# Scores and state products in halves of TensorE's array, and the chunk output made turned, in one bank with the carried part

## The reference

```python
x = silu(causal_conv(x_in @ Wx.T));  z = x_in @ Wz.T            # 512 channels
b = (x @ Wb.T).reshape(bsz, seq, 8, 64);  c = (x @ Wc.T).reshape(bsz, seq, 8, 64)
dt = softplus(x @ Wdt.T + b_dt);  a = -exp(log_a)
def step(state, (x_t, b_t, c_t, dt_t)):                         # over 1024 tokens
    state = exp(dt_t * a) * state + (dt_t * b_t)[..., None] * x_t[:, :, None, :]
    y_t = einsum('bhn,bhnp->bhp', c_t, state)
y = y + d_param * x;  y = (y - mean_head) / sqrt(var_head + eps) * gn_w + gn_b
out = (y * silu(z)) @ Wout.T
# second half: gelu(h @ (alpha1*sign(w1)).T + b1) @ (alpha2*sign(w2)).T + b2
```

## Time and profile before

| | |
|---|---|
| median of three runs | 1528.94 us (1528.52 to 1531.23) |
| the profiled execution | 1531.44 us, its span 1529.7 us |
| mean granted TensorE clock | 0.974 |
| TensorE busy | 1426.4 us, 93% of the span |
| its weight loads | 986.9 us, 65% |
| VectorE | 1092.1 us, 71% |
| ScalarE | 828.8 us, 54% |
| GpSimd | 439.2 us, 29% |

### The profile page before, as it was taken

How to read it: one execution, slowest core, us unless ns; L and a number is a source line. 1 busy time by engine, 2 the same in 40 slices (tenths; PEclk the granted TensorE clock), 3 DMA queues, 4 the chain that set the end, 5 groups by cost and what they waited for, 6 DMA issues and landing times.

```text
span 1529.7 us, 28256 instructions
## 1 busy us (share of the span) xinstructions
PE 1426.4 (93%) x9712; PEld 986.9 (65%) x9712; DVE 1092.1 (71%) x2424; ACT 828.8 (54%) x1718; POOL 439.2 (29%) x487
## 2 busy tenths in 40 slices
PE   4999999998999989999999999999899999999776
PEld 3484758676485856758577675867658585675654
DVE  5454786858777686876859678685877769586665
ACT  3555574555745475553746447454674547555231
POOL 2020242214331232313422134321333134321343
PEclk8899999999999999999999999999999999999888
DMA  6000000101000010100001010010100000000000
GB/s 225 1 15 1 15 1 1 42 1 44 1 15 28 2 44 1 42 1 16 29 1 43 1 44 1 2 42 1 44 1 17 26 1 28 1 28 1 28 1 28
DMA packets 33351, 33.22 MB, mean 22 GB/s; under 512 B 4888, under 2 KB 31640, under 8 KB 33184
## 3 DMA queue, kind: packets, MB, share of 16 engines
q1 hardware_dynamic: 33184, 31.11, 6.2%
HBM read 22.72 MB, written 8.39 MB: 20 GB/s over the span
## 4 chain that ended last, share of the span: by engine, by line
PE 66%; issue 14%; DVE 10%; POOL 5%; ACT 2%; SPq 1%; DMA 0%; POOLq 0%; DVEq 0%; ACTq 0%
PE bank L1291 20%; PE bank L1473 7%; PE bank L1460 7%; PE bank L1377 6%; PE bank L1410 5%; PE bank L1445 4%; PE bank L1389 4%; PE bank L1369 3%; PE bank L1397 3%; PE bank L1359 2%; PE bank L1361 2%; SPq L548 1%; PE bank L1301 1%; DVE un L937 1%; POOL yT L670 1%
## 5 line engine op out<-in xcount | busy, mean ns | idle before, releaser
L686 POOL TENSOR_TENSOR xdw<-xdt,decays 128x512 f32<-128x512 f32 x64 | 66.7, 1043 | 430.3 <-DVE xdt L1043 408.1
L1291 PE MATMUL bank<-sh,WbT 128*128 128x512 f16 x768 | 174.3, 383 | 10.3 <-DVE sh L967 10.1
L1291 PE MATMUL bank<-sh,WcT 128*128 128x512 f16 x768 | 175.5, 379 | 0.0
L881 ACT ACTIVATE yk<-bank,decays 128x64 f32<-128x64 f32 x512 | 112.1, 330 | 86.4 <-PE bank L1389 86.4
L962 DVE SCALAR_TENSOR_TENSOR xs<-xi,taps,xs 128x512 f32<-128x512 f32 x192 | 152.5, 805 | 8.7 <-ACT xs L787 4.4
L1473 PE MATMUL bank<-sign2T,hh 128*128 128x256 f16 x1024 | 151.2, 275 | 2.0 <-DVE hh L1157 2.0
L868 ACT ACTIVATE mt<-bank 128x512 f32<-128x512 f32 x128 | 69.5, 596 | 148.3 <-PE bank L1361 148.3
L1410 PE MATMUL bank<-xdt,mt 128*128 128x64 f32 x1024 | 142.9, 262 | 0.0
L1291 PEld LDWEIGHTS bank<-sh,WbT 128*128 128x128 f16 x768 | 73.6, 98 | 100.6 <-issue 14.5
L1410 PEld LDWEIGHTS bank<-xdt,mt 128*128 128x128 f32 x1024 | 134.9, 192 | 2.2
L1291 PEld LDWEIGHTS bank<-sh,WcT 128*128 128x128 f16 x768 | 75.1, 98 | 87.1
(11 more groups left out here) (182 smaller groups left out, 2755.1 us busy)
## 6 DMA issues: line engine op xcount, KB each, us to landing
xt<-L_attn_input_tensor_dram SPq DMA_DIRECT2D x16, 512.0 KB, 4.8
u<-L_attn_input_tensor_dram SPq DMA_DIRECT2D x16, 512.0 KB, 3.7
out_dram<-u SPq DMA_DIRECT2D x16, 512.0 KB, 3.0
yT<-in_L_ffn_w_dram SPq DMA_DIRECT2D x2, 1024.0 KB, 14.1
zs<-in_L_attn_Wb_dram SPq DMA_DIRECT2D x1, 1024.0 KB, 8.6
zs<-in_L_attn_Wc_dram SPq DMA_DIRECT2D x1, 1024.0 KB, 10.8
BT<-in_L_attn_Wx_dram SPq DMA_DIRECT2D x1, 512.0 KB, 4.7
BT<-in_L_attn_Wz_dram SPq DMA_DIRECT2D x1, 512.0 KB, 6.1
```

Source lines behind the costliest of these rows:

```text
L686: pool.tensor_tensor(xdw[n % 2][:, :, :], xdt[n % 2][:, :, :], per_head(decays[:, 1, q, :]), ALU.mult)\
L881: last = nc.scalar.activation(yk[n % 2][:, h, :], bank(t, ("YI", j, q))[:, h * HD:(h + 1) * HD], ACT.Copy, scale=decays[:, 0, q, h:h + 1])
L1291: mm = nc.tensor.matmul(bank(t, key)[:, :], w[i][:, k, cols(m)], v[h][:, k, :], start=(a == 0), stop=(a == len(terms) - 1))
```

## The change

It is made of these edits, all at once:

1. Scores: the eight S matmuls alternate between the two halves of rows (g = 0, 1 inside the loop over c); both banks are waited for before the first.
2. State product: St becomes eight matmuls, one a head, with 64 columns of weights and 64 moving, written to 64 partitions of the bank; the unused products go.
3. Chunk output: Y is made turned. The weights are `xdt` of a head (64 columns), `mt` moves (128 columns), the result goes to 64 partitions of the bank, and it is added to YI, which now is made turned too, with `state` as weights, in the same bank ("Y" begins in `carry`, ends in `back`).
4. Since YI can no longer be scaled by ScalarE afterwards, C is scaled before: a new fp16 matmul "E" of 512 columns over 64 rows at the end of `front`, an exponential of it on ScalarE into `Cd`, and a product with C on GpSimd, in front of YI.
5. `turn`, the eight scalings of L881, the addition of L1066 and the third of the decay sums (L1347) go; of VectorE's steps the addition to `yT` alone is left, and it is done in `back`.
6. The masks have other shapes: of_target halves, of_source doubles.

```diff
@@ turn_steps @@
-        steps += own(("turn", j, 0)) + [(who, "in_norm", nj)] + own(("front", j, 3)) + [(who, "xT", nj, 0)]
-        steps += tail(("end_stat", j)) + own(("carry", j, 2), ("back", j, 2), ("turn", j, 1)) + [(who, "xT", nj, 1)]
-        steps += tail(("end_root", j), ("end_norm", j)) + own(("carry", j, 3), ("turn", j, 2), ("back", j, 3))
+        steps += [(who, "in_norm", nj)] + own(("front", j, 3)) + [(who, "xT", nj, 0)]
+        steps += tail(("end_stat", j)) + own(("carry", j, 2), ("back", j, 2)) + [(who, "xT", nj, 1)]
+        steps += tail(("end_root", j), ("end_norm", j)) + own(("carry", j, 3), ("back", j, 3))
...
@@ GpSimd, front @@
+                pool.wait_ge(*E_out.count(t, n + 1))
+                pool.wait_ge(*C_out.count(t, (j + 1) * KI))
+                pool.tensor_tensor(Cd[n % 2][:, :, :], Cd[n % 2][:, :, :], CT[:, :, q * P:(q + 1) * P], ALU.mult)\
+                    .then_inc(Cd_out.sem, 1)
...
@@ ScalarE, front and carry @@
+                act.wait_ge(*full(t, ("E", j, q)))
+                act.wait_ge(*YI_done.count(s, ch(sj, sq) + 1))
+                nc.scalar.activation(Cd[n % 2][:, :, :].rearrange("p c t -> p (c t)"), bank(t, ("E", j, q))[:, :],
+                                     ACT.Exp).then_inc(E_out.sem, 1)
-            def carry(t, j, q):
...
-                for h in range(HEADS):
-                    last = nc.scalar.activation(yk[n % 2][:, h, :], bank(t, ("YI", j, q))[:, h * HD:(h + 1) * HD],
-                                                ACT.Copy, scale=decays[:, 0, q, h:h + 1])
...
@@ VectorE, back and turn @@
-                nc.vector.tensor_tensor(yk[n % 2][:, :, :], yk[n % 2][:, :, :], heads(bank(t, ("Y", j, q))[:, :]),
-                                        ALU.add).then_inc(yk_out.sem, 1)
-            def turn(t, j, q):
...
-                nc.vector.tensor_tensor(v, bank(t, ("YT", j, q))[:, :].rearrange("p (c t) -> p c t", c=KI), v,
+                nc.vector.tensor_tensor(v, bank(t, ("Y", j, q))[:, :].rearrange("p (c t) -> p c t", c=KI), v,
                                         ALU.add).then_inc(yT_out.sem, 1)
...
@@ TensorE, front @@
                 for g in range(HP):
-                    key = ("S", j, q, g)
-                    rows = slice(g * NS, (g + 1) * NS)
-                    pe.wait_ge(*empty(t, key))
-                    for c in range(KI):
+                    pe.wait_ge(*empty(t, ("S", j, q, g)))
+                for c in range(KI):
+                    for g in range(HP):
+                        key = ("S", j, q, g)
+                        rows = slice(g * NS, (g + 1) * NS)
                         mm = nc.tensor.matmul(bank(t, key)[:, cols(c)], BT[rows, c, cols(q)], CT[rows, c, cols(q)],
                                               start=True, stop=True)
...
+                key = ("E", j, q)
+                pe.wait_ge(*empty(t, key))
+                nc.tensor.matmul(bank(t, key)[:, :], of_source[0:HALF, q].rearrange("p g s -> p (g s)")[:, HALF:HALF + P],
+                                 of_target[0:HALF, :, :].rearrange("p c t -> p (c t)"), start=True, stop=True)\
+                    .then_inc(full_sem(t, key), 1)
...
@@ TensorE, carry @@
+                    mm = nc.tensor.matmul(bank(t, key)[:, cols(c)], state[:, c, :], Cd[r][:, c, :],
+                                          start=(c == 0), stop=False)
...
-                for c in range(KI):
-                    mm = nc.tensor.matmul(bank(t, key)[:, cols(c)], bt[r][:, cols(c)],
-                                          xdw[r][:, HP * c:HP * c + HP, :].rearrange("p h n -> p (h n)"),
-                                          start=True, stop=True)
+                for h in range(HEADS):
+                    rows = slice(h % HP * NS, (h % HP + 1) * NS)
+                    mm = nc.tensor.matmul(bank(t, key)[rows, h * HD:(h + 1) * HD], bt[r][:, h * NS:(h + 1) * NS],
+                                          xdw[r][:, h, :], start=True, stop=True)
...
@@ TensorE, back_products @@
-                    mm = nc.tensor.matmul(bank(t, key)[:, h * HD:(h + 1) * HD], mt[r][:, h % HP, h // HP, :],
-                                          xdt[r][:, h, :], start=True, stop=True)
+                    c, g = h // HP, h % HP
+                    mm = nc.tensor.matmul(bank(t, key)[g * HD:(g + 1) * HD, cols(c)], xdt[r][:, h, :], mt[r][:, g, c, :],
+                                          start=False, stop=(h >= HEADS - HP))
```

More of the change, by code:

```diff
@@ L152, in turn_steps @@
         if j == 0:
-            steps += own(("xi", 0, 0)) + tail(("turn", NJ - 1, NQ - 1)) + own(("xi", 0, 1), ("xi", 0, 2))
+            steps += own(("xi", 0, 0), ("xi", 0, 1), ("xi", 0, 2))
             steps += tail(("head_stat", NJ - 1, 1), ("gn_sum",)) + own(("xi", 0, 3), ("silu_table",))
@@ L162, in turn_steps @@
         else:
-            steps += own(("xi", 1, 0), ("xi", 1, 1), ("turn", 0, NQ - 1), ("conv", 1, 0), ("head_stat", 0, 1))
+            steps += own(("xi", 1, 0), ("xi", 1, 1), ("conv", 1, 0), ("head_stat", 0, 1))
             steps += own(("xi", 1, 2), ("conv", 1, 1), ("xi", 1, 3), ("silu_table",), ("z", 1, 0), ("z_in", 1, 0))
@@ L290, in mamba_sandwich_kernel @@
         bt = [sb(f"bt{r}", [P, HEADS * NS]) for r in range(2)]
-        yk = [sb(f"yk{r}", [P, HEADS, HD]) for r in range(2)]
+        Cd = [sb(f"Cd{r}", [P, KI, P]) for r in range(2)]
         state = sb("state", [P, KI, P])
@@ L341, in uses @@
                 heads_of = [[(name, *at, g) for g in range(HP)] for name in ("seg", "S")]
[L342 removed]
+                return [*heads_of[0], ("X", *at), ("Bt", *at), *heads_of[1], ("E", *at)]
             if kind == "carry":
[L344 to L346 removed]
+                return [("Y", *at), ("St", *at)]
             if kind == "uT":
                 return [("uT", *at, k) for k in range(KD)]
[L349 removed]
+            return [("gn",)] if kind == "gn_mean" else []
         own_keys, tail_keys, in_keys = [], [], []
@@ L353, in mamba_sandwich_kernel @@
             if kind == "back+O":
-                own_keys += uses("back", *at)
                 who, kind = "tail", "O"
@@ L1345, in decay_sums @@
                 pe.wait_ge(*empty(t, key))
-                for n, w in enumerate((upto, after, ones)):
+                for n, w in enumerate((after, ones)):
                     mm = nc.tensor.matmul(bank(t, key)[:, n * NQ * HEADS:(n + 1) * NQ * HEADS], w[:, :], da,
@@ L1383, in carry @@
                 r = n % 2
-                key = ("YI", j, q)
-                for need in latest(empty(t, key), st_out.count(t, n * HP) if n else st_zero.count(t, 1)):
+                key = ("Y", j, q)
+                for need in latest(empty(t, key), Cd_out.count(t, n + 1),
+                                   st_out.count(t, n * HP) if n else st_zero.count(t, 1)):
                     pe.wait_ge(*need)
                 for c in range(KI):
-                    mm = nc.tensor.matmul(bank(t, key)[:, cols(c)], CT[:, c, cols(q)], state[:, c, :],
-                                          start=True, stop=True)
-                mm.then_inc(full_sem(t, key), 1)
+                    mm = nc.tensor.matmul(bank(t, key)[:, cols(c)], state[:, c, :], Cd[r][:, c, :],
+                                          start=(c == 0), stop=False)
+                mm.then_inc(YI_done.sem, 1)
                 key = ("St", j, q)
@@ L1493, in _ @@
                 "xT": turn_input, "xi": project_x, "z": project_z, "dt": step_size, "B": project_b, "C": project_c,
-                "cums": running_sums, "sums": decay_sums, "front": front, "carry": carry, "back": back, "turn": turn, "gn_mean": head_means,
+                "cums": running_sums, "sums": decay_sums, "front": front, "carry": carry, "back": back, "gn_mean": head_means,
                 "Wo": attention_out, "uT": turn_middle, "H": hidden, "O": ffn_out,
```

117 lines of the change are left out of this document (49 added, 68 removed).

## The result

The changed kernel takes 1552.29 us (median of 4 runs, 1550.15 to 1553.46) against 1530.03 for the kernel before in the same call (4 runs, 1528.52 to 1531.23): ratio 1.0144, 95% interval 1.0127 to 1.0162. It is 22.3 us slower; 1538 was forecast. The profiled executions took 1531.4 and 1550.2 us, their spans are 1529.7 and 1548.3. That is 18.6 us between the spans; the rest of the 22.3 is the spread of the runs around them.

The account below looks back on a forecast made before the run. TensorE bounds among FFN products, VectorE behind them. 50 (first chunks) - 30 (VectorE-bound stretch) - 9 (batch 0) - 3 (tail) = +8 to +9 us on 1531.4, so 1538 us median; own range 1524 to 1556, whole range 1480 to 1568.

Parts of the forecast that it names:

- Entering and leaving a column half among whole-array matmuls: Output products among FFN products, 28 chunks: a head takes 0.68 us against 0.39, +2.2 us a chunk, +61 us.
- the small gains: First chunks up to the FFN products' end: scores, E, St and decay sums, -0.8 us a block, -11 us.
- Rival 1: Output products among FFN products: column halves cost no restart, +9 instead of +61, 1486 us; chance 0.22.
- rival 2: Column-half matmuls: they do not overlap and their loads are no shorter, 1567 us; chance 0.14.
- rival 4: Among FFN products, 28 chunks: sparse pairs bring the 1.2 GHz level, about +3 us each, 1620 us; chance 0.03.
- Scores, E, St, Y: TensorE's gains or losses per chunk: scores -0.55 us, E +0.22, St -0.1, Y alone -0.69 in 36 chunks.
- VectorE bounds behind the FFN products: FFN products' end to next B projection: VectorE loses four additions, 2.4 us, plus 0.1 slack, seven times.
- Rival 3: Behind the FFN products: VectorE is not the bound, 3.7 us gained 13 times, -18 us, 1520 us; chance 0.11.
- (c): E matmul, +0.22 us; its exponential and C product are covered, GpSimd's state decay starts about 1 us later.
- batch 0: Two blocks without FFN between: -5.7 us on TensorE, of which VectorE gives 4.5; -9 us.
- The loop's end: Across the loop's or a batch's end, six times: -2.0 us each; 0.8 of the Y gain becomes longer gap.
- the end: The tail after the last FFN products: its first wait loses a scaling and an addition, -3 us.

Follow-up runs that it names:

- experiment 1: Changed kernel with a chunk's output products in one piece ahead of its FFN products, not spread among them: 1480.72 us, ratio 0.9672.
- experiment 2: Changed kernel with output products spread among the FFN products by pairs of heads, not single heads: 1498.37 us, ratio 0.9781.
- experiment 5: Kernel before with only the scores alternating between the row halves: 1512.16 us, ratio 0.9878.
- experiment 6: Kernel before with only the chunk state products St in column halves: 1526.43 us, ratio 0.9975.
- Experiment 4: Changed kernel with the scores of chunks 2 and 3 back in the old order, one half after the other: 1556.76 us, ratio 1.0163.
- experiment 3: Kernel before with a chunk's output products in one piece ahead of its FFN products: 1539.74 us, ratio 1.0062.
- the variant with xT last: Second variant of experiment 10: its first, plus last input transposes behind the last output products in each second block: 1483.04 us, ratio 0.9688.
- experiment 7: GpSimd's state decay of chunks 0 and 1 ahead of the next C product: 1472.96 us on experiment 1's kernel, 1547.58 us on the changed kernel.
- experiment 8: Experiment 1's kernel with the next block's input statistics (and their root) elsewhere in the queues: 1489.86 us, ratio 0.9742.
- experiment 10: First variant: experiment 7's faster kernel, with chunk 2's decay before chunk 3's C product and its state addition before the FFN statistics: 1476.36 us, ratio 0.9642.
- experiment 9: Experiment 1's kernel with the output products of each batch's last chunk one half after the other: 1476.33 us, ratio 0.9646.

## Why the prediction was right or wrong

**Entering and leaving a column half among whole-array matmuls (+61, with the small gains +50):** right, in mechanism and size. A head takes 0.69 us against the forecast 0.68, and the stretch grew by 3.6 us a block as the sum has it. Experiments 1 and 2 took 72 and 54 us away, where 74 and 54 were expected. That the small gains add up is a little luck. From the state product to the end of the FFN product a chunk grew by 1.96 us and not by 2.1, and up to the first state product a block gained nothing (7.75 against 7.73) where 0.25 was forecast. The rule of the Trainium skill that it was set beside (TensorEngine Tiling (Array Packing), Key Properties: a change of mode drains) agrees, for columns as for rows, in that each visit costs: 0.26 us in experiment 2. Rival 1 is out. So is rival 2, since column halves overlap (sixteen output records in 0.98 us, not 1.73), and rival 4, since the granted clock was 1.00 among the FFN products.

One reading of the earlier trace rows is loose: of the two S matmuls that span 0.49 us the first is 0.37 long and not 0.27. The second starts 0.21 behind it all the same, so the price of entering stands.

**Scores, E, St, Y:** scores gained 0.64 and not 0.55 us, E cost 0.31 and not 0.22. Together that is -0.33 as forecast; the 0.09 for leaving the half, which the sum had behind the scores, now stands behind E, and without E (experiment 5) the scores gain 0.55. St among whole-array matmuls is worth 0.08 net (experiment 6; forecast 0.1). Experiments 4 and 5 show the scores' gain where it was put: in chunks 1 and 2, and 0.14 or nothing in chunk 3. In chunk 0 it is 0.1 us of loss. The reading of the Trainium skill, TensorE: Matmul & The Clock Gate, Packing small matmuls, by which column halves share their rows and their loads could not pass, asks for 0.86 us (an estimate, 16 x 0.053); St takes 0.51 here and 0.61 in experiment 6, so the measurement decides for overlap.

**VectorE bounds behind the FFN products:** right. It is -2.51 us a block against -2.5, of which 2.28 come up to the B projection, where the forecast looked, and 0.22 behind it. Experiment 4 gives TensorE 0.6 us more to do there and the time doesn't move. Rival 3 is out.

**The step that failed** is in (c): "behind them in the queue waits GpSimd's state decay, which then starts about 1 us later and still ends before VectorE's statistics let its addition go". In VectorE's queue the state addition of chunk 1 stands ahead of the statistics, not behind them, and VectorE waited for the decay already in the kernel before (1.55 us at 95.81). The C product took 1.27 us, not the 1.04 of the earlier trace rows. In steady batches the FFN products covered most of what came of it. Batch 0 has none, and there the bank for B's transposes waits for what is behind it. The forecast gave batch 0 -9 us and it got -1.1; with the decay first it is -6.1.

The cause of the last 3 us stays open, with two candidates in the traces. With the decay first TensorE still waits 4.3 us for that bank in batch 0, against 1.3 in the kernel before. And the granted clock is 0.5 for 3.4 us of batch 0 before (126.5 to 129.9), for 10.3 us after (123.5 to 130.4 and 167.9 to 171.3) and for as long again with the decay first in the changed kernel. At half the clock, 6.9 us more can hold TensorE back by 3.4 us at most (an estimate).

**The loop's end** is the second step that failed. The sign was right and the size was not: "0.8 of the Y gain turns into a longer gap". The gap grew by 2.1 us (1.65 to 3.72): 0.96 because sixteen queued records now last 0.77 us and not 1.73, as argued, and 1.1 because the branch itself took 4.5 to 5.0 us in the changed kernel and 3.4 to 3.7 in the kernel before, a term that the sum doesn't have. The five loop ends gained 1.5 us each where 2.0 were forecast. Where batch 7 begins, without a loop's branch, nothing was gained at all: 67.12 us against 67.08. From xi to B, with the granted clock in the third last column, before and after:
```profile
1266.00:1286.60 20.60, 18.77 (x86) 11.07 (x86) 19.12 (x42) 16.49 (x30) 6.59 (x6) 1.00 0.16 52
```
```profile
1283.00:1304.40 21.40, 19.76 (x82) 11.12 (x83) 17.65 (x39) 16.52 (x30) 6.33 (x6) 0.92 0.15 49
```
TensorE's idle time in front had grown from 1.01 to 2.31 us, and behind it stood the 1.2 GHz level, which the kernel before had not met there: 1.0 us. That the longer gap brought it is not shown, since other kernels here have the same gap without it (last section).

In all, +8.5 us forecast in the span, +18.6 measured: 7.9 from batch 0 and 4.6 from these six stretches, 0.6 from the large term, less 2.2 of the setup and 0.7 of the end. Without the two misses it would have been 1540.

## What to carry to other kernels

Packing an array in halves pays in runs of such matmuls: order them so that partial and whole matmuls don't alternate, because each visit cost 0.25 to 0.3 us here whether it held 2, 4 or 16 records, and a visit of one half alone also gives up the overlap of the two. Where a helper mixes two streams to hide weight loads, ask again whether the mix pays once one stream changes its form. And a new operation on a side engine is priced by what stands behind it in that engine's queue in the stretch with the least cover (here batch 0); a step that is moved moves in every engine's queue.

## What the runs showed of the hardware

The branch at the end of the loop takes 3.3 to 3.9 us in some executions of it and 4.5 to 5.1 in others. The kernel before, its variants of experiments 3, 5 and 6, and the variant with xT last had only short ones, 3.4 to 3.7. The changed kernel, experiments 2, 7 and 8 and the first variant of experiment 10 had only long ones; experiments 1, 4 and 9 had both. In each of the 34 short ones one 16 KB packet of instructions starts while the branch runs, 0.9 to 1.6 us after its start. In each of the 36 long ones two do, the second 0.9 to 1.5 us after the start of the branch. The length goes with the pace of the last sixteen records: where they take 1.1 us or more, 29 of 30 were short, where they take 0.77 us, 5 of 40. Why is not settled, and experiment 1 has four short ones at 0.77. A long one costs 1.2 us more, and so 6 us here.

The clock didn't fall at the same gap each time. In the kernel of experiment 1 the first loop end (idle 2.54 us) and the start of batch 7 (2.31 us) were followed by full clock, the third loop end by the lower level, 1.2 us more for the same work:
```profile
352.40:372.70 20.30, 18.41 (x82) 10.65 (x82) 17.61 (x39) 16.48 (x29) 6.26 (x6) 1.00 0.25 80
1223.50:1243.20 19.70, 18.10 (x82) 10.76 (x82) 17.63 (x39) 16.45 (x29) 6.37 (x6) 1.00 0.16 54
699.40:720.90 21.50, 19.79 (x82) 11.18 (x82) 17.62 (x39) 16.49 (x29) 6.28 (x6) 0.92 0.23 76
```
In the changed kernel the lower level followed the 2.31 us in front of batch 7, and in the kernel of experiment 6 it followed 1.14 us there. So changes of 1 to 2 us at such places come and go between variants that don't touch them.
